# A four-layer convolution chain on one core: weight slices and sums at the begin reordered, side work spread over the slots, last image of the main stage by halves

## The chip, the core and the metric

The kernel runs on one core of a Trainium2 chip. The metric is the device time of one execution in microseconds (us). TensorE (PE) multiplies, VectorE (DVE) and ScalarE (ACT) do the elementwise work, GpSimd (POOL) does a few small chains, SyncE (SP) issues most of the DMAs. Each engine runs its own list of instructions in the order in which the code writes them, and waits on semaphores.

## The reference

The input x has 16 images of 32 channels and 28 x 28 pixels. Four layers follow each other.

```
def ternarize(w):
    delta = 0.7 * mean|w|;  mask = |w| > delta
    alpha = sum(|w| * mask) / sum(mask)
    return alpha * sign(w) * mask
# layer 0: 32 -> 192 -> 192 -> 32 channels
h = relu6(bn(conv1x1(x, ternarize(w1)), ...))
h = relu6(bn(conv3x3(h, ternarize(w2)), ...))
h = bn(conv1x1(h, ternarize(w3)), ...)
y = x + h
# layer 1: two 3x3 convolutions, input and weights rounded to 8 bits with a step from the
#          maximum over the whole tensor, batch norms, relu, residual
# layers 2 and 3: 3x3 convolution, bias, batch norm, relu; a whole channel of an image
#          is zeroed where its maximum is under 0.001
```

The mean of |w2| is a sum over 192 x 192 x 9 weights, and no weight of w2 can be made ternary before it is known. The step of each 8-bit rounding in layer 1 needs the maximum over all 16 images, so layer 1 can't start before the last image of layer 0 is done.

## The kernel before, in words

**Data.** Four images are stacked in the 128 partitions; c counts the four groups, g the image in a group, and j = 4c + g is an image of 0 to 15. The 192 hidden channels are two blocks, 0 to 127 ("a") and 128 to 191 ("b", 64 wide, of which two row sets share the 128 columns as a "pair"). `big` holds the raw weights of w2 (`w2ar` for the input channels 0 to 127, `w2br` for the other 64, once in each half of the partitions).

**Begin.** DMAs bring w2a in three slices, w2b, w1, w3, x and the batch-norm parameters. ACT sums |w2a| by slices (L684), then |w2b| (L687), and adds the three slice sums up (L690). PE sums over the partitions by a product with ones (`total`, L396). DVE derives the threshold (`thr_ready`), makes w2 ternary (`w2_rows`, `w2_transforms`, `w2_rest`) and forms the transformed weights wu and wub. POOL works out the batch-norm factors once the parameters land (`inv_ready`). The input is split exactly into three bf16 parts (`split` on DVE, `x_high` on ACT), and SP copies the parts of each image under each other (`spread`), so that one product over 96 rows is the expansion. Image 0 is expanded directly (L537).

**Main stage.** Each engine runs `slot(c, g)` 16 times. In a slot PE issues four quarters of the expansion of image j + 2 (`expand`, L421, all through PSUM bank 6, so that each has to wait until ACT has read the one before, `relu_exp`, L703), the outer row products of image j (`outer(0)`, `outer(3)`, L454), the middle ones of image j + 1 (`middle`, L444), and the pairs `pair_outer(j)` (L475) and `pair_middle(j+1)` (L464). In the first slot of a group it also projects the group before (`project`, L490). DVE's slot begins with `rows_03(j+1)` (L1061) and goes on with `seed_pair(j)` (L1081), the clamps of image j - 1 (`upper_a` L1086, `lower_a` L1091, `upper_b` L1096, `lower_b` L1101), the fixed-point split of image j + 2 (`grid` L1038, `fine` L1045/L1047), `seed_rows(j+1)` (L1072/L1073: they write the banks into which `outer` of the next slot accumulates) and `rows_12(j+2)` (L1055/L1056). ACT's slot is:

```
relu_exp(j+2, 0); relu_b(j-1); copy_y(j); [x_high of the next group]
relu_exp(j+2, 1); relu_exp(j+2, 2); coarse(j+2, 0)
relu_a(j); relu_exp(j+2, 3); copy_m1(j+1); coarse(j+2, 1); [add_shift(c) if g == 1]
```

Work that isn't any image's own is called **side work** below: the splits of groups 1 to 3, `w3_rest` (w3 made ternary), `scales` (the factor alpha), the maxima of the layer-1 to layer-3 weights (L1201 to L1204) with the transposes that spread them, and `integers` (L809/L813, the rounded weights of layer 1). Before, DVE does `w3_rest` and `split(1)` ahead of its first slot, and nearly all else behind its slots 0, 1 and 2. Slots 4 to 11 are a hardware loop.

**End of the main stage.** Slot 15 computes its outer rows and its pair. ACT reads both row blocks in one instruction (`relu_a`), DVE clamps the whole image, PE projects both halves of the pixels, and `residual` (L1108, L1111) adds x and takes maxima. Then `step(0)` finds the global maximum: DVE L1242, PE `largest` (L587), DVE L1244 to L1247, and layer 1 begins. `keep_warm` (L407) issues products whose result isn't used.

**Layers 1 to 3.** Two quantized 3x3 convolutions (L597), with `step(1)` between them, then two layers over stacked copies (L632). The order is written by hand throughout.

## Time and profile before

| what | us |
|---|---|
| median of 3 runs | 285.79 |
| those runs | 286.43, 285.79, 283.64 |
| the profiled execution's own time | 283.94 |
| its span in the profile | 282.1 |
| PE busy | 243.8 |
| DVE busy | 243.4 |
| ACT busy | 192.1 |
| POOL busy | 11.9 |

The span leaves out about 1.8 us of the profiled execution's own time. Busy time is a mean over very different stages: the main stage, from 33 to 207 us, has PE busy nearly all the time, while the begin and the turn to layer 1 are chains of short steps.

### The profile page before, as it was taken

The numbers are of one execution on the slowest core, as the hardware profiler recorded it, in microseconds if no ns is written. First come the engines' busy times: TensorE is split into PE (matmuls) and PEld (weight loads), VectorE is DVE, ScalarE is ACT, GpSimd is POOL, SyncE is SP. The second block draws the span as 40 slices with busy tenths as digits, with TensorE's granted clock in tenths as the row PEclk, the third lists the DMA queues.
The fourth block names the chain that finished last, engine by engine and source line by source line (L and its number), as shares of the span: only waits on it lengthen the run. The fifth ranks groups of instructions, "written<-read, shape, count | busy, mean of one in ns | idle before, by whom it ended". The sixth has DMA issues, their size and how long they took to land.

```text
span 282.1 us, 5680 instructions
## 1 busy us (share of the span) xinstructions
PE 243.8 (86%) x2138; PEld 132.1 (47%) x2138; DVE 243.4 (86%) x458; ACT 192.1 (68%) x283; POOL 11.9 (4%) x24
## 2 busy tenths in 40 slices
PE   0455979788999999999999999999977999789963
PEld 0222435344655455555455555455533555445531
DVE  6589996999999999999799999797658848999873
ACT  3686756587767578768378777778423728998942
POOL 6600000000000000000000000000000000000021
PEclk9999979999999999999999999999999999999998
DMA  7922003121200000000000000000000000275254
GB/s 209 281 75 73 1 14 75 28 59 36 50 2 1 2 0 3 0 2 0 0 0 0 0 0 0 1 2 0 2 0 2 0 0 4 59 163 109 62 149 171
DMA packets 6902, 11.55 MB, mean 41 GB/s; under 512 B 2144, under 2 KB 5216, under 8 KB 6880
## 3 DMA queue, kind: packets, MB, share of 16 engines
q1 hardware_dynamic: 6608, 10.77, 14.3%
q10 hardware_dynamic: 272, 0.49, 0.7%
q8 instruction: 14, 0.23, 0.3%
q14 instruction: 8, 0.07, 0.1%
HBM read 4.04 MB, written 1.61 MB: 20 GB/s over the span
## 4 chain that ended last, share of the span: by engine, by line
PE 61%; DVE 15%; DMA 7%; ACT 7%; issue 5%; SPq 4%; DVEq 0%; ACTq 0%
PE ps L454 14%; PE ps L444 14%; PE ps L475 8%; PE ps L464 7%; PE ps L597 4%; PE ps L632 3%; PE ps L421 3%; SPq L311 3%; DMA big<-big 3%; DMA big<-w2a_in 2%; PE ps L490 2%; DMA big<-part 2%; PE ps L537 1%; DVE ug L1038 1%; ACT ra L703 1%
## 5 line engine op out<-in xcount | busy, mean ns | idle before, releaser
L703 ACT ACTIVATE ra<-ps,bn 128x392 f32<-128x392 f32 x64 | 43.3, 677 | 28.7 <-PE ps L421 26.1
L725 ACT ACTIVATE hs<-ug,magic 128x784 f16<-128x784 f16 x32 | 30.2, 949 | 17.3 <-DVE ug L1038 17.3
L454 PE MATMUL ps<-vv,w2at 128*128 128x392 f16 x192 | 39.0, 338 | 0.5 <-DVE ps L1072 0.5
L444 PE MATMUL ps<-vv,wu 128*128 128x392 f16 x180 | 36.4, 336 | 0.0
L421 PE MATMUL ps<-xk,w1t 96*128 (+1 forms) x60 | 20.9, 348 | 11.9 <-ACT ra L703 11.9
L632 PE MATMUL ps<-big,wst 128*32 128x392 f16 (+2 forms) x576 | 25.5, 333 | 6.0 <-DMA big<-big 4.3
L597 PE MATMUL ps<-qi,wqi 128*128 128x392 bf16 x144 | 25.0, 333 | 1.0 <-ACT qi L838 1.0
L454 PEld LDWEIGHTS ps<-vv,w2at 128*128 128x128 f16 x192 | 18.4, 98 | 14.2 <-issue 1.6
L1061 DVE TENSOR_TENSOR vv<-hs 128x2520 f16<-128x2520 f16 x16 | 23.4, 1461 | 0.0
L444 PEld LDWEIGHTS ps<-vv,wu 128*128 128x128 f16 x180 | 17.5, 97 | 12.3 <-issue 0.4
L632 PEld LDWEIGHTS ps<-big,wst 128*32 128x32 f16 x576 | 14.7, 96 | 16.9 <-DMA big<-big 5.8
L454 PE MATMUL ps<-vv,w2bt 128*128 128x392 f16 x96 | 22.2, 340 | 0.0
L444 PE MATMUL ps<-vv,wub 128*128 128x392 f16 x90 | 20.4, 333 | 0.0
L475 PE MATMUL ps<-vv,w2at 128*64 128x392 f16 x192 | 19.7, 338 | 0.0
L1038 DVE TENSOR_SCALAR ug<-ra 128x784 f16<-128x784 f32 x32 | 17.9, 563 | 2.0 <-ACT ra L703 1.5
L597 PEld LDWEIGHTS ps<-qi,wqi 128*128 128x128 bf16 x144 | 13.8, 97 | 12.2 <-ACT qi L838 1.8
L464 PE MATMUL ps<-vv,wun 128*64 128x392 f16 x96 | 19.4, 336 | 0.0
L464 PE MATMUL ps<-vv,wu 128*64 128x392 f16 x96 | 19.4, 336 | 0.0
L870 ACT COPY big<-part 32x900 f16<-32x900 f16 x20 | 18.9, 943 | 0.5 <-DVE part L1373 0.2
L731 ACT ACTIVATE r2a<-ps,bn 128x784 f32<-128x784 f32 x16 | 16.1, 1003 | 4.4 <-PE ps L454 2.2
L421 PEld LDWEIGHTS ps<-xk,w1t 96*128 96x128 bf16 x60 | 5.8, 96 | 24.4 <-ACT ra L703 18.5
L838 ACT ACTIVATE qi<-ra,magic 128x420 bf16<-128x420 f32 (+1 forms) x16 | 9.0, 615 | 12.0 <-DVE ra L1254 12.0
(213 smaller groups left out, 461.5 us busy)
## 6 DMA issues: line engine op xcount, KB each, us to landing
xk<-xpart SPq DMA_DIRECT2D x45, 49.0 KB, 1.9
big<-big SPq DMA_DIRECT2D x4, 450.0 KB, 3.9
xin<-x_in SPq DMA_DIRECT2D x4, 392.0 KB, 7.2
big<-part SPq DMA_DIRECT2D x26, 56.2 KB, 2.4
y_out<-xin SPq DMA_DIRECT2D x3, 392.0 KB, 2.4
big<-w2a_in SPq DMA_DIRECT2D x3, 288.0 KB, 5.7
big<-w2b_in ACTq DMA_DIRECT2D x1, 432.0 KB, 5.9
big<-w2b_in SPq DMA_DIRECT2D x1, 432.0 KB, 6.8
```

Source lines behind the costliest of these rows:

```text
L421: nc.tensor.matmul(ps[:, bank, :HALF], (w1t[:, 0:P], w1t[:, P:P + 2 * HB])[two], xk[:, j, HALF * h:HALF * h + HALF], start=True, stop=True ...
L444: i = nc.tensor.matmul(ps[:, PBANK[k], :HALF], weights(s, k, dx, False), moving(s, k, dx, b), start=(s == 0 and dx == 0), stop=(s == 2 and ...
L454: i = nc.tensor.matmul(ps[:, PBANK[k], :HALF], weights(s, k, dx, False), moving(s, k, dx, b), start=False, stop=(s == 2 and dx == 2), skip ...
L464: i = nc.tensor.matmul(ps[HB * q:HB * q + HB, 4, :HALF], weights(s, k, dx, True), moving(s, k, dx, b), start=(s == 0 and dx == 0), stop=(s ...
L475: i = nc.tensor.matmul(ps[HB * q:HB * q + HB, 5, :HALF], weights(s, k, dx, True), moving(s, k, dx, b), start=False, stop=(s == 2 and dx == 2),
L597: i = nc.tensor.matmul(ps[:, bank + h, :HALF], wqi[:, k, t, :], qi[:, c, r0:r0 + HALF_ROWS, dx:dx + W], start=(t == 0), stop=(t == TAPS - 1))
L632: i = nc.tensor.matmul(ps[C * g:C * g + C, bank + h, :W * (rows.stop - rows.start)], wst[:, layer, C * t:C * t + C], kst[:, KBUF[layer][c] ...
L703: nc.scalar.activation(dst[:, HALF * h:HALF * h + HALF], ps[:, bank, :HALF], ACT.Relu, bias=bn[:, BSH, at:at + 1], scale=bn[:, BSC, at:at ...
L725: nc.scalar.activation(inner(hs[:, 2 * two]), img(ug[:, two, :]), ACT.Identity, bias=magic[:, 2:3]).then_inc(hh_ready, 1)
L870: ins = nc.scalar.copy(kst[C * k:C * k + C, KBUF[layer][c], g], part[C * g:C * g + C, layer, c % 2, k])
L1038: ts(ug[:, two, :], ra[:, two, :], CAP, GRID, ALU.min, ALU.add).then_inc(ug_ready, 1)
L1061: tt(vv[:, b, :, 0].rearrange("p s h w -> p s (h w)"), hs[:, :, 0:H, :].rearrange("p s h w -> p s (h w)"), hs[:, :, 2:H + 2, :].rearrange( ...
```

## The change

At the begin: x of group 0 is loaded first; the third slice of w2a goes through ACT's queue with w2b in three slices; w3 and the second copy of w2b wait until the first weights have landed, and x of groups 1 to 3 is loaded behind the spread of group 0. The halves of |w2b| are summed by ACT and DVE, and one product with ones takes five columns of partial sums, which DVE then adds up. The expansions of image 1 go to four banks and no longer wait for each other, and 18 products without use follow (`warm`). POOL clears `qi`, which DVE cleared before. ACT copies w1 (L841) and does its square sum of w2b ahead of `copy_m1(0)`.

In the main stage the loop is written out, and the side work is placed anew: `split` is two pieces, `split_first` (xrest) behind or in one slot and `split_second` (xpart) behind the next; `w3_rest` follows slot 1; the w3 scale (`scales_3`) is a step of its own; the weight maxima, the transposes and `split` of group 3 move to later slots, and the two `integers` stand ahead of slot 12 and behind it, where they stood behind slots 12 and 13.

At the end: the last pair's outer products go to bank 3, ahead of the last image's `outer(3)`, which is then PE's last; ACT and DVE treat the last image by halves; the small product for layer 1's scales moves ahead of `residual`. In layer 1 the last image of the first convolution has 18 and 10 rows in place of 14 and 14, and the clamp by 1e-8 becomes a ninth column of the maxima.

```diff
         @block.sync
+            sp.dma_start(xin[:, 0, :], x[:, 0, :]).then_inc(s_x[0], 16)
             for k in range(2):
                 dy = slice(3 * HID * k, 3 * HID * k + 3 * HID)
                 sp.dma_start(w2ar[:, dy], w2a[:, dy]).then_inc(s_w2a[k], 16)
-            sp.dma_start(xin[:, 0, :], x[:, 0, :]).then_inc(s_x[0], 16)
-            sp.dma_start(w2ar[:, 6 * HID:], w2a[:, 6 * HID:]).then_inc(s_w2a[2], 16)
+            sp.wait_ge(s_w2a[2], 16)
+            sp.wait_ge(s_w2b, 48)
             sp.dma_start(w3r[:, 0, :], w3[0:P]).then_inc(s_w3, 16)
...
         @block.tensor
-            pe.wait_ge(a_sum, 1)
-            total(3, 1, col[:, SUMS + 1:SUMS + 2], col[:, SB + 1:SB + 2])
+            pe.wait_ge(b_sum, 1)
+            pe.wait_ge(a_abs, 4)
+            total(3, 5, col[:, W2S:W2S + 5])
...
+            pe.wait_ge(thr_ready, 1)
+            pe.wait_ge(rb_ready, 2)
+            for n in range(4):
+                expand(1, n, bank=(0, 1, 5, 6)[n])
+            warm(WARM)
...
+            j = B - 1
+            outer(0, j, j % 2)
+            pair_outer(j, j % 2, bank=PBANK[2])
+            outer(3, j, j % 2)
             pe.wait_ge(rb_ready, 2 * B)
-            keep_warm(3, 4)
-            project(NCH - 1, 0, (0, 1), late=2)
-            project(NCH - 1, 1, (0, 1), bank=6, late=2)
-            keep_warm(4, 4)
-            project(NCH - 1, 0, (2, 3), late=2)
-            project(NCH - 1, 1, (2, 3), bank=6, late=2)
+            project(NCH - 1, 0, end=True)
+            project(NCH - 1, 1, (2, 3, 0, 1), bank=6, end=True)
...
         @block.scalar
+            slot(0, 0, first=True)
+            slot(0, 1, first=True, split=1)
+            x_high(2, 0)
+            slot(0, 2, first=True)
+            slot(0, 3, first=True, split=2)
+            act.wait_ge(pool_zeroed, 6)
+            slot(1, 0)
+            slot(1, 1)
+            x_high(3, 0)
+            slot(1, 2)
+            slot(1, 3, split=3)
+            slot(2, 0)
...
+            slot(2, 3)
             act.wait_ge(ws_ready, 1)
...
+            integers(0)
+            slot(NCH - 1, 0, last=True)
+            integers(1)
+            slot(NCH - 1, 1, last=True)
+            slot(NCH - 1, 2, last=True)
+            copy_y(B - 1)
+            relu_b(B - 2)
+            relu_half(B - 1, 0)
+            relu_b(B - 1, bank=PBANK[2])
+            relu_half(B - 1, 1)
...
         @block.vector
...
+            dve.wait_ge(s_w2b, 48)
+            nc.vector.tensor_reduce(c1(W2S + 4, HB), w2br[0:HB, TAPS * HID // 2:], AX.X, ALU.add,
+                                    apply_absolute_value=True).then_inc(b_sum, 1)
...
+            link(nc.vector.tensor_reduce(c1(TMP), ps[:, TOTAL_BANK[3], 24:29], AX.X, ALU.add))
...
-            w3_rest()
-            rows_12(1, 1)
-            split(1)
-            slot(0, 0, first=True)
-            split(2)
...
+            rows_12(1, 1)
+            slot(0, 0, first=True)
+            split_second(1)
+            slot(0, 1, first=True)
             w3_rest()
...
+            slot(0, 2, first=True)
+            split_first(2)
+            slot(0, 3, first=True)
+            split_second(2)
+            scales_3()
+            slot(1, 0)
+            slot(1, 1)
...
+            sizes(0)
+            slot(1, 2)
+            split_first(3)
+            slot(1, 3)
+            split_second(3)
+            slot(2, 0)
+            sizes(1)
...
+            seed_pair(j, bank=PBANK[2])
...
+            upper_half(j, g, 0)
+            lower_half(j, g, 0)
+            upper_b(j, g)
+            lower_b(j, g)
+            upper_half(j, g, 1)
+            lower_half(j, g, 1)
+            PQ, PC = 66, 68
+            link(tt(c1(PQ, w=2), c1(SW, w=2), bn[:, BSC, BNQ1:BNQ2 + 1], ALU.mult))
+            ts(c1(PQ, w=2), c1(PQ, w=2), 1.0 / XQ, None, ALU.mult)
             residual(NCH - 1, 0)
...
-                link(ts(c1(GM + k), c1(GM + k), 1e-8, None, ALU.max))
```

**DVE ahead of its first slot and in it.** The two splits' names are xrest and xpart, `seed_pair(0)` is the line `ps<-cy,ps`. Before:

```order
L1056 TENSOR_TENSOR vv<-hs 128x3x14x30
L970 TENSOR_TENSOR xrest<-xin 128x784
L972 TENSOR_TENSOR xpart<-xrest 128x784
L1061 TENSOR_TENSOR vv<-hs 128x3x840
L1081 TENSOR_TENSOR ps<-cy,ps 128x392
L1167 TENSOR_TENSOR col<-ps,col 128x1
```

Now, from the same place (L1137 is the old L1056, L1142 the old L1061):

```order
L1137 TENSOR_TENSOR vv<-hs 128x3x14x30
L1142 TENSOR_TENSOR vv<-hs 128x3x840
L1164 TENSOR_TENSOR ps<-cy,ps 128x392
L1259 TENSOR_TENSOR col<-ps,col 128x1
L1261 TENSOR_TENSOR col<-col,ps 128x1
L1262 TENSOR_SCALAR col<-ps 128x1
L1263 RECIPROCAL col<-col 128x1
L1264 TENSOR_TENSOR col<-col 128x1
L1270 TENSOR_SCALAR bn<-bn,col 128x2
L1119 TENSOR_SCALAR ug<-ra 128x784
L1041 TENSOR_TENSOR xrest<-xin 128x784
```

Both halves of the split of group 1, and `w3_rest`, no longer stand ahead of the first slot; one half stands inside it, the other behind it.

**ACT at the turn from slot 11 to slot 12.** `wqq` and `wqi` are the rounded weights of layer 1. Before, they stood behind slot 12:

```order
L709 COPY c1a<-ps 128x392
L725 ACTIVATE hs<-ug,magic 128x28x28
L809 ACTIVATE wqq<-wqr,magic,col 128x288
L813 ACTIVATE wqi<-wqq,magic 32x9x32 x4
L703 ACTIVATE ra<-ps,bn 128x392
```

Now the same pair of instructions stands ahead of slot 12 as well as behind it, and no longer behind slot 13:

```order
L757 COPY c1a<-ps 128x392
L773 ACTIVATE hs<-ug,magic 128x28x28
L872 ACTIVATE wqq<-wqr,magic,col 128x288
L876 ACTIVATE wqi<-wqq,magic 32x9x32 x4
L751 ACTIVATE ra<-ps,bn 128x392
```

**DVE at the end of the main stage.** `h2a` and `h2b` are the clamped last image. Before, the last lines up to the first `residual`:

```order
L1086 TENSOR_SCALAR h2a<-r2a 128x784
L1096 TENSOR_SCALAR h2b<-r2b 128x392
L1091 SCALAR_TENSOR_TENSOR h2a<-r2a,h2a 128x784
L1101 SCALAR_TENSOR_TENSOR h2b<-r2b,h2b 128x392
L1108 SCALAR_TENSOR_TENSOR y<-ps,bn,xin 128x14x28
```

Now:

```order
L1180 TENSOR_SCALAR h2a<-r2a 128x392
L1186 SCALAR_TENSOR_TENSOR h2a<-r2a,h2a 128x392
L1191 TENSOR_SCALAR h2b<-r2b 128x392
L1196 SCALAR_TENSOR_TENSOR h2b<-r2b,h2b 128x392
L1180 TENSOR_SCALAR h2a<-r2a 128x392
L1186 SCALAR_TENSOR_TENSOR h2a<-r2a,h2a 128x392
L1358 TENSOR_TENSOR col<-col,bn 128x2
L1359 TENSOR_SCALAR col<-col 128x2
L1203 SCALAR_TENSOR_TENSOR y<-ps,bn,xin 128x14x28
```

The first half and the pair's clamp stand ahead of the second half, which alone depends on PE's last products.

## Rows read from the trace of the kernel before

**Rows 1.** Windows: PE's slots 0, 3, 8: length, busy PE PEld DVE ACT POOL, PEclk, DMA

```profile
33.45:47.82 14.37, 12.41 (x82) 6.50 (x81) 12.00 (x33) 8.87 (x14) 0.00 (x0) 0.88 0.15 37
...
73.90:84.15 10.25, 10.25 (x78) 5.71 (x77) 9.87 (x20) 7.43 (x11) 0.00 (x0) 1.00 0.03 8
...
127.17:139.34 12.17, 12.17 (x111) 6.14 (x109) 10.03 (x16) 7.21 (x11) 0.00 (x0) 1.00 0.00 0
```

**Rows 2.** Chain that ended last, the begin (start, us, what)

```profile
2.10 6.92 DMA big<-w2a_in
```

**Rows 3.** Page, GB/s of the DMA engines in 40 slices of 7.05 us

```profile
GB/s 209 281 75 73 1 14 75 28 59 36 50 2 1 2 0 3 0 2 0 0 0 0 0 0 0 1 2 0 2 0 2 0 0 4 59 163 109 62 149 171
```

**Rows 4.** Timeline of the begin (start, us, engine, what, idle before and its end)

```profile
2.22 3.10 POOL L363 MEMSET part<- 128x3600 f32 x1
8.62 0.33 POOL L369 TENSOR_SCALAR bn<-par 128x9 f32<-128x9 f32 x1 [3.30 <-DMA par<-params_in]
9.73 1.63 ACT L687 ACTIVATE big<-big 64x1728 f32<-64x1728 f32 x1
13.10 0.23 DVE L981 TENSOR_SCALAR bn<-bn,col 128x2 f32<-128x2 f32 x1 [2.20 <-POOL bn L377]
13.68 0.80 DVE L1001 TENSOR_SCALAR big<-big,col 128x1152 f16<-128x1152 f32 x1
...
25.64 4.13 PE L553 MATMUL ps<-vv,wu 128*128 128x392 f16 x12
...
29.75 0.25 DVE L1015 TENSOR_SCALAR wubn<-wub 128x192 f16<-128x192 f16 x1
```

**Rows 5.** Timeline of DVE: `rows_03`, the entry of its slots 0, 3, 4 and 5

```profile
39.99 1.46 DVE L1061 TENSOR_TENSOR vv<-hs 128x2520 f16<-128x2520 f16 x1
77.13 1.45 DVE L1061 TENSOR_TENSOR vv<-hs 128x2520 f16<-128x2520 f16 x1
86.72 1.46 DVE L1061 TENSOR_TENSOR vv<-hs 128x2520 f16<-128x2520 f16 x1
97.92 1.46 DVE L1061 TENSOR_TENSOR vv<-hs 128x2520 f16<-128x2520 f16 x1
```

**Rows 6.** Timeline of ACT at the turn from slot 3 to slot 4

```profile
83.19 0.95 ACT L725 ACTIVATE hs<-ug,magic 128x784 f16<-128x784 f16 x1 [0.26 <-DVE ug L1038]
84.62 0.68 ACT L703 ACTIVATE ra<-ps,bn 128x392 f32<-128x392 f32 x1 [0.47 <-PE ps L421]
86.91 0.68 ACT L703 ACTIVATE ra<-ps,bn 128x392 f32<-128x392 f32 x1
```

**Rows 7.** Side work: groups of lines (busy, mean ns, idle), then timeline of ACT

```profile
L970 DVE TENSOR_TENSOR xrest<-xin 128x784 f32<-128x784 f32 x3 | 2.9, 963 | 0.0
...
48.27 0.83 ACT L677 COPY xpart<-xin 128x784 bf16<-128x784 bf16 x1
...
179.11 2.17 ACT L813 ACTIVATE wqi<-wqq,magic 32x288 bf16<-32x288 f32 x4
```

**Rows 8.** Windows: PE idle in slot 0, and 2 us later (columns as in Rows 1, PE alone)

```profile
35.35:37.12 1.77, 0.00 (x0) 1.00 0.00 0
39.00:40.00 1.00, 1.00 (x5) 0.50 0.00 0
```

**Rows 9.** Timeline of the end of the main stage

```profile
206.42 0.68 PE L475 MATMUL ps<-vv,w2bt 128*64 128x392 f16 x6
206.50 0.57 DVE L1086 TENSOR_SCALAR h2a<-r2a 128x784 f16<-128x784 f32 x1 [0.31 <-ACT r2a L731]
...
209.25 0.85 PE L490 MATMUL ps<-h2a,w3t 128*32 128x392 f16 x16 [1.55 <-DVE h2a L1091]
...
211.37 0.62 DVE L1108 SCALAR_TENSOR_TENSOR y<-ps,bn,xin 128x392 f32<-128x392 f32 x1 [1.78 <-PE ps L490]
...
214.19 0.46 PE L587 MATMUL ps<-ident,mx 128*128 128x128 f32 x2 [1.42 <-DVE mx L1242]
...
215.01 0.15 DVE L1245 TENSOR_SCALAR col<-col 128x1 f32<-128x1 f32 x1
```

More of the change, by code:

```diff
@@ L478, in pair_outer, with project @@
                 i.then_inc(convb_done, 1)
-            def project(c, h, steps=(0, 1, 2, 3), bank=7, late=1):
+            def project(c, h, steps=(0, 1, 2, 3), bank=7, end=False):
                 wait(pe, y0_ready, 2 * c + h if bank == 7 else 0)
@@ L658, in _ @@
             act.dma_start(w1r[:], w1).then_inc(s_w1, 16)
-            act.dma_start(w2br[0:HB, :], w2b).then_inc(s_w2b, 16)
             act.dma_start(par[:], params).then_inc(s_par, 16)
+            act.dma_start(w2ar[:, 6 * HID:], w2a[:, 6 * HID:]).then_inc(s_w2a[2], 16)
+            for k in range(3):
+                dy = slice(3 * HID * k, 3 * HID * k + 3 * HID)
+                act.dma_start(w2br[0:HB, dy], w2b[:, dy]).then_inc(s_w2b, 16)
             n = [0]
@@ L746, in add_shift, with slot @@
                                      bias=bn[:, BSH, BN3:BN3 + 1]).then_inc(xs_ready, 1)
-            def slot(c, g, first=False, last=False):
+            def slot(c, g, first=False, last=False, split=None):
                 j = c * G + g
                 begin = first and g == 0
-                end = last and g == G - 1
                 ahead = not last or g < G - 2
@@ L764, in slot @@
                     copy_y(j)
-                if first and g < NCH - 1:
-                    x_high(g + 1, 1)
+                if split is not None:
+                    x_high(split, 1)
                 if ahead:
@@ L769, in slot @@
                     relu_exp(j + 2, 2)
+                if begin:
+                    copy_m1(j + 1)
+                if ahead:
                     coarse(j + 2, 0)
                 if begin:
-                    copy_m1(j + 1)
+                    relu_exp(j + 2, 3)
                     act.wait_ge(bn_ready, 1)
                 relu_a(j)
-                if ahead:
+                if ahead and not begin:
                     relu_exp(j + 2, 3)
-                if not end and not begin:
+                if not begin:
                     copy_m1(j + 1)
@@ L782, in slot @@
                     add_shift(c)
+            x_high(0, 1)
+            act.wait_ge(w1_ready, 1)
+            for k in (1, 2):
+                i = nc.scalar.copy(w1t[C * k:C * k + C, :], w1t[0:C, :])
+            i.then_inc(w1_ready, 1)
             act.wait_ge(bn1_ready, 1)
@@ L1115, in slot @@
                 begin = first and g == 0
-                end = last and g == G - 1
                 ahead = not last or g < G - 2
-                if not end:
-                    rows_03(j + 1, (g + 1) % 2)
+                rows_03(j + 1, (g + 1) % 2)
                 seed_pair(j)
@@ L1139, in slot @@
                     grid(j + 2, 1)
-                if not end:
-                    seed_rows(j + 1)
+                seed_rows(j + 1)
                 if g == 0 and not first:
@@ L1205, in _ @@
             i.then_inc(mxt_go, 1)
-            slot(0, 1, first=True)
-            split(3)
+            slot(2, 1)
             dve.wait_ge(mxt_done, 1)
```

338 lines of the change are left out of this document (188 added, 150 removed).

## The prediction

> **What bounds the kernel now.** I read the windows per slot first. From slot 3 on PE is busy without a break: slot 3 takes 10.25 us with 10.25 busy, slot 8, which also projects, 12.17 of 12.17 [rows 1]. There a faster DVE or ACT gains nothing. Slots 0 to 2 are different: slot 0 takes 14.37 with 12.41 busy, at a mean clock of 0.88, and DVE is busy 12.00 against 9.87 in slot 3 [rows 1]. They are long because DVE does side work there. Against three slots of 10.27 the stage loses some 9.6 us (slots 0 to 2 last from 33.45 to 73.90, 40.45 in all [rows 1]). The begin, before PE's slot 0 at 33.45, is a chain: the last slice of w2a lands at 9.0 [rows 2], ACT sums, PE adds over partitions, DVE gets the threshold and starts on w2 at 13.68; the last transformed weight is written at 30.0 [rows 4]. The end is a chain too: PE's last product of the stage ends at 207.1, `largest` stands at 214.19, with only 0.85-us pieces of PE between [rows 9].
>
> So three things can move the time: when the first slot begins, how much side work PE has to wait for, and the 7.1 us at the end.
>
> **The begin.** What must land for the threshold is x of group 0 (0.40 MB), w2a (0.88), one copy of w2b (0.44) and small things, 1.77 MB. Before, it shared the engines with w3, the second w2b and 1.2 MB of x. The page shows 209 GB/s in the first slice of 7.05 us (1.47 MB) and 281 in the second [rows 3], so 1.77 MB are through at 7.05 + 0.30/0.281 = 8.1 us. Then ACT sums the last slice, a third of the columns of L687 (1.63) and so about 0.7 with the read-out, and half of w2b, 0.8 + 0.2: to 10.0, where L687 ended at 11.4 [rows 4]. From there to DVE's first step on w2 it took 2.3 us (to 13.68): ACT's sum of sums, two products, six short DVE steps. Now the sum of sums and one product are gone and the sums of |w3| stand elsewhere, some 1.1 less, but the expansion's scale, worked out in ACT's shadow before, and one more DVE step come in, 0.8: 2.0, so DVE starts on w2 at 12.0, 1.7 earlier. POOL must not be late: it clears `part` until 5.3 and now `qi` (half as many elements, half of 3.10), to 6.9; its chain from 8.62 to 13.0 lasts 4.4 [rows 4], so 11.3. Hence the gain lies between 0.7 (slice still at 9.0) and 2.1 (POOL ends last). The second w2b and groups 1 to 3 land later, but their readers come after 22 us; a DMA of SP is late only if `spread(0)` moves past the end of image 0's expansion, which it meets within a microsecond.
>
> The Trainium skill, page "DMA: Bandwidth & Descriptors", section "Anatomy of one DMA", gives about 2 us fixed plus bytes at 436 GB/s. By that the weights would be there at some 6.8 us, and the gain would be POOL's bound, 2.1; the slices of the page of the profile, at 209 and 281 GB/s, don't agree, and I go by them.
>
> Between there and the first slot, image 0's expansion starts as soon as the product is out (it stood behind it before), which saves DVE a short wait, and the two sums of |w3| cost 0.35 in the middle of the w2 chain. The transformed weights end at 28.3 in place of 30.0. PE then has six products and `pair_middle` to do, 2.6 us at the fast level: its slot 0 starts at 30.9. DVE entered slot 0 at 39.99 [rows 5]; off that come `split(1)`, two instructions of 0.96 [rows 7], `w3_rest`, eight short steps at some 0.19 with their gaps (0.15 each, [rows 9]), and the 1.7: 34.9.
>
> **The clock.** PE's 12 products of image 0 take 4.13 us at 25.64 [rows 4], 0.33 each, against 0.17 in full slots (78 products in 10.25 us, 36 of them two at a time [rows 1]): the 1.2 GHz level. The 18 products (6 us, from 16.5 to 22.5) end where DVE has image 0's rows ready, and should bring the 2.4 GHz level: 2 us of PE saved, but DVE's w2b chain follows until 28.3, so the saving turns into idle time. In that idle time of 3 us the level may fall back: a pause of 1.77 us at 35.35 is followed by a granted clock of 0.50 at 39 us [rows 8]. The Trainium skill, page "TensorE: Matmul & The Clock Gate", section "What's actually happening", says an idle array drops to half rate; that speaks against this placement of the useless products. By the row PE would lose up to 1.7 us between 28 and 33. I count it at nothing, since DVE, entering at 34.9, is the later one in slot 0; with its cover gone it costs 1.7.
>
> **The slots.** Two rules, both from the turn 3 to 4. DVE without side work takes 9.6 us a slot (77.13 to 86.72 [rows 5]); a `residual`, 1.2, comes on top in the first two slots of groups 1 to 3. PE's slot j+1 can't keep pace before DVE's entry to slot j plus 6.5: ACT's `coarse` ends 7.0 after the entry (83.19 + 0.95 - 77.13 [rows 5, 6]), then ACT needs 2.97 from 84.62 to 87.59 for four steps before PE's third quarter of the expansion, which stands 3.47 into PE's slot [rows 6]. What ACT does in between comes on top: `x_high` 0.85, `add_shift` the same size (I take 0.93), `integers` 2.17 and the rounding ahead of it, 2.8 [rows 7]. DVE's seeds give the same bound. Entries of DVE, with the side work in brackets: slot 1 at 45.8 (clamps absent, six scale steps 1.15, split 1.9, a short wait for ACT), 2 at 56.9 (w3 1.5), 3 at 67.5 (0.97), 4 at 79.0 (0.97, 0.95), 5 at 89.8, 6 at 101.5 (two maxima over 288 columns, estimated at 0.9 from 0.96 for 784), 7 at 112.1, 8 at 122.7 (0.97 each), 9 at 134.8 (1.3), 10 at 146.1 (0.5), 11 at 156.9 (1.15). PE, at 10.3 a slot and 12.2 in slots 4, 8 and 12: slot 1 at 42.5; slot 2 not at 53.2 but at 45.8 + 6.5 + 0.93 + 0.83 = 54.1; slot 3 at 64.4; 4 at 75.2 (with the w3 product, 0.5); 5 at 87.4; 6 at 99.3 for 97.7 (residual, `add_shift`, `x_high`); 7 at 109.6; 8 at 119.9; 9 at 132.1; 10 at 143.4 for 142.4; 11 at 154.0; slot 12 at 156.9 + 6.5 + 2.8 = 166.2 for 164.3, because `integers(0)` now stands ahead of it, where ACT has no pause that long. Before it was 170.16: eight full slots of 10.27 and two of 12.2 after 73.90, less what is rounded. From there PE is full again. **Gain in the main stage 4.0**, of which 2.5 are the begin's. If no side work delayed PE at all, slot 12 would start at 160.7, a gain of 9.4; that is the upper bound. The lower one is the begin's 0.7 alone. I take 4.0, because both rules come from full slots.
>
> The loop written out costs nothing: slots outside and inside it take the same time [rows 1].
>
> **The end.** PE's work is the same and ends at the same distance, with `outer(3)` of image 15 last. Counted from that end: ACT reads 392 columns 0.7; DVE clamps 0.4 and 0.6 (half of the full-image instructions), to 1.7; two short steps 0.4, to 2.1; two residuals as before. Before, the first residual stood 4.3 behind PE's end and `largest` another 2.8 [rows 9]; now 2.1 and 2.6, since the two short steps no longer stand between. 4.7 in place of 7.1: **2.4**, between 1.8 and 2.8. The project's first half needs the pair's clamp, which is done 0.1 after PE's end. Clamping by 1e-8 goes from both maximum chains, 0.19 each (a step of 0.15 with its gap [rows 9]): 0.4. The last image's 18 and 10 rows shorten the last ACT and DVE pieces of the first convolution by some 0.1 each: 0.2.
>
> **Sum.** 4.0 + 2.4 + 0.4 + 0.2 = 7.0. The profiled execution took 283.94 by itself (span 282.1), so 276.9; the runs shown stand at 283.64, 285.79 and 286.43, and with the profiled one their mean is 285.0. I put the forecast at 285.0 - 7.0 = 278.0; against the median alone it would be 278.8.
>
> **Rivals.** First, the side work is all covered: ACT's and DVE's bounds are looser than the turn 3 to 4 tells, and PE is the only bound from slot 1. Then the stage gains up to 9.4, and the time is 272.6 to 275. For it: DVE idles a little in every full slot, 9.87 busy of 10.25. Against: with DVE entering four microseconds behind PE, ACT has no pause left. Chance 0.17.
>
> Second, DVE lags more than I count and only begin and end pay, 1.7 + 3.0: 280.3. For it: 12 slots carry extra steps, each with a semaphore. Chance 0.15.
>
> Third, the clock: the level stays at 1.2 GHz through slot 0 and its 18 products of `outer`, 1.5 more than counted, and reaches DVE by `seed_rows(1)`: 279.5. Chance 0.08.
>
> Fourth, the change doesn't do what it says: the slices land no earlier, as ACT's queue issues the third slice of w2a behind w1 and the parameters. Gain of the begin 0.7, time 279.0. Chance 0.07.
>
> Fifth, slower: the side work now lies in slots where PE had no break. Put off there are the last split piece of group 2, the w3 scale, the maxima, the split of group 3 and the weight scales, 0.97 + 0.95 + 2.2 + 1.9 + 0.5 + 1.15 = 7.7 us of DVE. It decides from a DVE slot of 10.27 upward, PE's own length: then each of them is paid in full while slots 0 to 2 stay as they are, 285.0 + 7.7 - 4.7 = 288.0. DVE's 9.6 speaks against it. Chance 0.03.
>
> The forecast itself, 276.3 to 279.9 by its bounds, has 0.50. The range from 273.5 to 281.5 leaves out the best part of the first rival, the slower one, and some error of the base. A measurement of this kernel tells about 1% from no change, here 2.9 us. Faster by more than that (below 282.9): 0.9; within 0.07; slower 0.03.
>
> **What would show it.** DVE starts on w2 near 12.0; PE's slot 0 near 31, DVE's entry near 35; the products of image 0 at 0.17 each; PE waits for ACT (the expansion) at slots 2, 6, 10 and 12 by one to two microseconds and not elsewhere; slot 12 at 166; `largest` 4.7 behind PE's last `outer`. It is wrong if PE waits in most slots, or if DVE's slot without side work isn't 9.6.

## The result, and the profile after

| what | us |
|---|---|
| the changed kernel, median of 4 runs | 275.84 (276.95, 275.83, 274.72, 275.85) |
| the kernel before, median of 4 runs beside it | 285.99 (283.64 to 286.43) |
| ratio, 95% interval | 0.966 (0.962 to 0.970) |
| the profiled execution of the changed kernel | 276.95, span 275.0 |

The kernel is faster by 3.4%. Forecast were 278.0 (273.5 to 281.5) and faster. The kernel was run six more times later; over all ten runs its median is 276.20, and that is the number with which the experiments below are compared.

The page of the changed kernel, busy share, clock and GB/s in 40 slices of 6.9 us:

```profile
PE   0585889999999999999999997999988999889973
DVE  5899979999999999999899998799678858999893
PEclk9999599999999999999999999999999999999998
GB/s 235 90 108 215 9 1 0 54 37 0 2 22 68 1 0 4 0 2 66 23 2 4 0 0 0 4 2 0 2 0 1 2 0 0 61 153 109 102 132 175
```

The loads are seen to be in another order: 235 GB/s in the first slice, 90 in the second, 215 in the fourth, where the page of before has 209 and 281 and then falls to 75 [rows 3]. The row of the clock has a digit 5 near 30 us; the row of before has a 7 near 38 us, and 9 near 30.

Windows of PE's slots 0, 3, 8 and 12, then PE's pause at the begin and the stretch behind it (length, busy PE PEld DVE ACT POOL, clock, DMA):

```profile
33.45:45.45 12.00, 11.23 (x83) 6.33 (x81) 9.43 (x19) 6.65 (x10) 0.00 (x0) 0.96 0.00 1
67.10:78.02 10.92, 10.40 (x79) 5.70 (x78) 10.72 (x16) 7.96 (x12) 0.00 (x0) 1.00 0.01 2
121.84:133.99 12.15, 12.15 (x110) 6.15 (x109) 11.23 (x18) 7.42 (x11) 0.00 (x0) 1.00 0.20 50
165.41:179.47 14.06, 12.50 (x111) 6.13 (x109) 11.44 (x18) 12.09 (x21) 0.00 (x0) 1.00 0.01 2
25.15:28.30 3.15, 0.00 (x1) 0.01 (x1) 3.01 (x8) 1.61 (x3) 0.00 (x0) 0.88 0.28 72
30.00:34.00 4.00, 4.00 (x22) 1.71 (x21) 3.93 (x7) 2.51 (x5) 0.00 (x0) 0.50 0.03 6
```

Slot 0 lasts 12.00 in place of 14.37, slot 3 10.92 in place of 10.25, slot 8 the same [rows 1]. The side work has left the first slots and is seen in the later ones as DVE's 10.72 busy of 10.92. Slot 12 is now the worst: 14.06 with 12.50 busy, and PE waits in it for ACT, which is busy 12.09. PE's slot 0 starts at 33.45, to the hundredth where it stood before, although the last transformed weight came 1.8 us sooner: of the four microseconds from 30 to 34 all were at the granted clock of 0.50, the 1.2 GHz level.

Timeline of the begin and of slot 0 (start, us, engine, what, idle before):

```profile
8.79 0.92 ACT L734 ACTIVATE big<-big 64x864 f32<-64x864 f32 x1 [0.45 <-DMA big<-w2b_in]
...
11.93 0.81 DVE L1082 TENSOR_SCALAR big<-big,col 128x1152 f16<-128x1152 f32 x1
...
17.27 4.87 PE L572 MATMUL ps<-part 128*128 128x392 f16 x18
...
22.91 2.24 PE L589 MATMUL ps<-vv,wu 128*128 128x392 f16 x12 [0.43 <-DVE vv L1137]
...
27.99 0.25 DVE L1096 TENSOR_SCALAR wubn<-wub 128x192 f16<-128x192 f16 x1
...
28.30 2.14 PE L589 MATMUL ps<-vv,wub 128*128 128x392 f16 x6 [3.15 <-DVE wubn L1096]
...
34.96 1.46 DVE L1142 TENSOR_TENSOR vv<-hs 128x2520 f16<-128x2520 f16 x1
...
37.72 0.16 DVE L1259 TENSOR_TENSOR col<-ps,col 128x1 f32<-128x1 f32 x1 [0.82 <-PE ps L411]
...
41.57 0.98 DVE L1128 SCALAR_TENSOR_TENSOR hs<-ra,hs 128x784 f16<-128x784 f32 x1 [1.30 <-ACT hs L773]
...
47.63 1.46 DVE L1142 TENSOR_TENSOR vv<-hs 128x2520 f16<-128x2520 f16 x1
```

DVE starts on w2 at 11.93 (13.68 before [rows 4]), ends the transformed weights at 28.24 (30.0) and enters slot 0 at 34.96 (39.99 [rows 5]). The 12 products of image 0 take 2.24 us in place of 4.13, but behind them PE now idles 3.15 us until the last weights are there, where it idled 0.29 before. In slot 0 DVE waits twice: 0.82 us for PE's `total` (L411), which stands behind PE's first outer products, and 1.30 us for ACT's `coarse` (L773), ahead of which ACT has waited 2.66 and 1.05 us for PE's expansion.

Waits of PE, 33 to 203 us, in one line: 3.9 us in six pieces, two of them in slot 12 (total, number of waits, longest).

```profile
PE ps L438 <- ACT ra L751: 3.9, 6, 1.2
```

Timeline of the end of the main stage:

```profile
203.67 0.68 PE L471 MATMUL ps<-vv,w2bt 128*128 128x392 f16 x3
...
205.50 0.57 DVE L1186 SCALAR_TENSOR_TENSOR h2a<-r2a,h2a 128x392 f16<-128x392 f32 x1
...
206.12 0.52 PE L509 MATMUL ps<-h2a,w3t 128*32 128x392 f16 x8 [0.86 <-DVE h2a L1186]
...
206.26 0.63 DVE L1203 SCALAR_TENSOR_TENSOR y<-ps,bn,xin 128x392 f32<-128x392 f32 x1
...
208.95 0.46 PE L626 MATMUL ps<-ident,mx 128*128 128x128 f32 x2 [0.88 <-DVE mx L1368]
```

From PE's last outer product (204.35) to `largest` it is 4.6 us, where it was 7.1 [rows 9].

**Where the time came from**, by spans: before 282.1 in its profile, with its slot 13 at 182.3, `largest` at 214.2 and 67.9 behind that. The changed kernel's slot 13 stands at 179.5 in its first profile, but at 178.2, 178.5 and 179.1 in three others with the same begin and slots (below). So the stage gives 2.8 by the first and 3.7 by the mean of the three, the end 2.4 (from slot 13 to `largest` 31.9 before, 29.5 now), and the stretch behind the first maximum 1.9 to 2.1.

### The profile page after: what moved, and what is told of

Read it like the earlier page. It is cut to its first block, busy times and chain, and to the rows that moved or that the text cites. A ratio compares the mean times of both kernels' runs of the same rounds, so it can differ in the third digit from the quotient of the medians.

```text
span 275.0 us, 5586 instructions
## 1 busy us (share of the span) xinstructions
PE 245.5 (89%) x2151; PEld 133.5 (49%) x2151; DVE 244.4 (89%) x460; ACT 192.3 (70%) x285; POOL 14.2 (5%) x26
## 4 chain that ended last, share of the span: by engine, by line
PE 56%; DVE 19%; ACT 9%; issue 6%; DMA 6%; SPq 1%; ACTq 1%; DVEq 0%
PE ps L461 14%; PE ps L471 10%; PE ps L492 8%; PE ps L481 8%; PE ps L636 5%; PE ps L671 3%; PE ps L438 3%; DMA big<-big 3%; ACT ra L751 2%; DMA big<-w2b_in 2%; ACT hs L773 2%; PE ps L509 2%; PE ps L563 1%; DVE hs L1126 1%; DVE ug L1119 1%
## 5 line engine op out<-in xcount | busy, mean ns | idle before, releaser
L773 ACT ACTIVATE hs<-ug,magic 128x784 f16<-128x784 f16 x32 | 30.2, 949 | 12.6 <-DVE ug L1119 12.6
L636 PE MATMUL ps<-qi,wqi 128*128 128x392 bf16 (+2 forms) x144 | 25.0, 333 | 0.7 <-ACT qi L913 0.7
L438 PE MATMUL ps<-xk,w1t 96*128 96x392 bf16 x60 | 20.3, 349 | 5.1 <-ACT ra L751 5.0
L1142 DVE TENSOR_TENSOR vv<-hs 128x2520 f16<-128x2520 f16 x16 | 23.4, 1461 | 0.0
L481 PE MATMUL ps<-vv,wun 128*64 128x392 f16 x96 | 20.4, 349 | 0.0
L481 PE MATMUL ps<-vv,wu 128*64 128x392 f16 x96 | 20.3, 348 | 0.0
L779 ACT ACTIVATE r2a<-ps,bn 128x784 f32<-128x784 f32 x15 | 15.1, 1003 | 3.7 <-DVE h2a L1174 3.7
L1128 DVE SCALAR_TENSOR_TENSOR hs<-ra,hs 128x784 f16<-128x784 f32 x16 | 15.6, 972 | 1.3 <-ACT hs L773 1.3
L1126 DVE SCALAR_TENSOR_TENSOR hs<-ra,hs 64x784 f16<-64x784 f32 x16 | 15.6, 976 | 0.9
```

The lines of the kernel that those rows point to most:

```text
L438: nc.tensor.matmul(ps[:, bank, :HALF], (w1t[:, 0:P], w1t[:, P:P + 2 * HB])[two], xk[:, j, HALF * h:HALF * h + HALF], start=True, stop=True ...
L481: i = nc.tensor.matmul(ps[HB * q:HB * q + HB, 4, :HALF], weights(s, k, dx, True), moving(s, k, dx, b), start=(s == 0 and dx == 0), stop=(s ...
L636: i = nc.tensor.matmul(ps[:, bank + h, :W * rows], wqi[:, k, t, :], qi[:, c, r + dy:r + dy + rows, dx:dx + W], start=(t == 0), stop=(t == ...
L773: nc.scalar.activation(inner(hs[:, 2 * two]), img(ug[:, two, :]), ACT.Identity, bias=magic[:, 2:3]).then_inc(hh_ready, 1)
L1142: tt(vv[:, b, :, 0].rearrange("p s h w -> p s (h w)"), hs[:, :, 0:H, :].rearrange("p s h w -> p s (h w)"), hs[:, :, 2:H + 2, :].rearrange( ...
```

## The experiments

All but a0_same, c_both and b_before are single edits of the changed kernel. The table has all runs but the kernel before; ratios are to the runs of the kernel before on the same chip in the same group (medians 285.14, 285.22 and 286.03).

| kernel | median us | ratio, 95% interval | against 276.20 |
|---|---|---|---|
| a0_same | 276.60 | 0.971 (0.968 to 0.974) | +0.4 |
| t_bridge | 274.92 | 0.964 (0.961 to 0.967) | -1.3 |
| t_nowarm | 275.80 | 0.968 (0.964 to 0.972) | -0.4 |
| t_integers | 275.23 | 0.966 (0.963 to 0.969) | -1.0 |
| u_end | 278.69 | 0.977 (0.974 to 0.980) | +2.5 |
| u_side | 278.35 | 0.977 (0.974 to 0.980) | +2.2 |
| u_layer1 | 276.86 | 0.974 (0.971 to 0.977) | +0.7 |
| u_load | 278.77 | 0.979 (0.976 to 0.982) | +2.6 |
| c_both | 273.15 | 0.956 (0.953 to 0.959) | -3.1 |

### The same kernel again

> The changed kernel itself, unaltered, as the base for the others of this group on the same chip. Both theories: 274.7 to 277.0, ratio to the kernel before 0.962 to 0.970. Rival reading of its first profile (a fall of the clock in slot 0 is rare and the usual run has none): the mean granted clock is over 0.995 in most runs; the other reading (it falls in every run): 0.985 to 0.990 in most.

Six runs of 275.44 to 277.19, median 276.60, at mean clocks of 0.984 to 0.994. So the fall of the clock isn't rare: in all six runs the mean is under 0.995, and the second of my two readings is nearer. Of the first four runs of this kernel one had a mean of 0.999, and it was the fastest of the ten (274.72). The mean counts falls at the kernel's end as well, so only a profile tells where one lies. The fall at the begin isn't equally long: in the first profile it slows the six products behind the pause and all of `pair_middle` (28.3 to 33.4 us), here it comes only behind the six products, and DVE goes from slot 0 to slot 1 in 11.52 us, 35.69 to 47.21, where it took 12.67. It doesn't wait for `total`, and 1.06 us for `coarse`. The ratio, 0.971, lies just above the 0.970 that was expected.

### 18 more products in the pause: t_bridge

```diff
                 if s == 2:
+                    warm(18)
                     pe.wait_ge(w2_ready, 3)
```

> Edit: 18 more products without use between the second and the third group of image 0's middle products, where PE of the changed kernel idles 3.15 us (25.15 to 28.30) ahead of a stretch of 6.8 us at a granted clock of 0.50. Theory A (DVE leads in slot 0, so the clock's fall costs nothing): within 0.5 us of the changed kernel. Theory B (the half-rate stretch holds up seed_rows(1) and so DVE's entry to slot 1, 47.63 where 45.8 was forecast, and that is carried to the end): PE's slot 0 starts at 31.5 or earlier with the clock at 1.00, DVE's slot 1 near 46, and the time is 1 to 2.5 us less.

1.3 us less than the ten runs, clocks 0.996 to 1.000. Theory B holds. Timeline of PE and DVE in this kernel:

```profile
26.50 3.15 PE L572 MATMUL ps<-part 128*128 128x392 f16 x18
...
29.80 1.22 PE L590 MATMUL ps<-vv,wub 128*128 128x392 f16 x6 [0.16 <-DVE wubn L1097]
...
36.41 1.46 DVE L1143 TENSOR_TENSOR vv<-hs 128x2520 f16<-128x2520 f16 x1
...
47.00 1.46 DVE L1143 TENSOR_TENSOR vv<-hs 128x2520 f16<-128x2520 f16 x1
```

The six products behind the pause take 1.22 us in place of 2.14, and slot 0 of DVE 10.59 in place of 12.67 and 11.52. The theory's outcome holds, its path doesn't: DVE waits 0.10 us ahead of `seed_rows(1)` here and 0.11 in the changed kernel. What goes away is the wait for `total` (0.82) and nearly all of the wait for `coarse` (1.30, here 0.14). My figures for the absolute times missed: slot 0 at 32.63, slot 1 of DVE at 47.00. In this execution the second slice of w2a landed late (ACT began on it at 9.37, in the first profile of the changed kernel at 6.91), which set the whole begin back by 1.5; the other five spans are 272.7 to 273.2 beside 274.1 here. `c_both`, below, shows the same edit with an early slice.

### No warm products at all: t_nowarm

```diff
-WARM = 18
+WARM = 0
```

> Edit: the 18 products without use are taken out. Theory A (they buy image 0's products at 0.17 each, but that time turns into idle time): image 0's 12 products take 0.33 each again, and the time is within 0.5 us of the changed kernel. Theory B (without them the clock rises later and slot 0 is slower still): 1 to 2 us more. Theory C (they cause the fall, since without them PE isn't granted the full rate before its pause and the climb comes once, in slot 0, as before): time 0 to 1 less.

0.4 less than the ten runs, 0.8 less than a0_same, 0.9 more than t_bridge. The timeline of PE:

```profile
23.11 4.08 PE L589 MATMUL ps<-vv,wu 128*128 128x392 f16 x12 [2.55 <-DVE vv L1137]
28.49 2.14 PE L589 MATMUL ps<-vv,wub 128*128 128x392 f16 x6 [1.31 <-DVE wubn L1096]
```

The 12 products are slow again and end 1.3 us ahead of the last weights: they were never on the path. PE climbs once, at about 32 us, as before, and its slot 0 starts at 32.98, 0.47 ahead of the first profile of the changed kernel. So the 18 products of the change bought nothing that these runs can tell: what they saved turned into a pause, and the pause cost the level. That is the first half of theory A and the mechanism of theory C; of B there is nothing.

### The end as it was: u_end

```diff
             outer(0, j, j % 2)
-            pair_outer(j, j % 2, bank=PBANK[2])
             outer(3, j, j % 2)
+            pair_outer(j, j % 2)
...
-            seed_pair(j, bank=PBANK[2])
+            seed_pair(j)
...
-            upper_half(j, g, 0)
-            lower_half(j, g, 0)
+            upper_a(j, g)
             upper_b(j, g)
+            lower_a(j, g)
             lower_b(j, g)
...
```

> Edit: the end of the main stage alone is put back as it was (last image whole, outer(3) ahead of its pair, keep-warm products, the small product for layer 1's scales behind residual). Theory A (the end's 2.4 us are a chain that nothing else covers): largest stands 7.1 behind PE's last product in place of 4.6, and the time is 2.3 to 2.7 more. Theory B (part of it came from the begin or the slots, or is taken back by layer 1): 0 to 1.5 more.

+2.5 by medians. The slots are those of the changed kernel (slot 13 at 178.47), `largest` stands at 210.35, 31.88 behind it; in a0_same it is 29.48 (179.06 to 208.54). That is 2.4, the sum of the prediction. Theory A. The waits that come back, from the timeline of PE in this kernel:

```profile
205.41 0.85 PE L628 MATMUL ps<-h2a,w3t 128*32 128x392 f16 x16 [1.55 <-DVE h2a L1189]
...
210.35 0.46 PE L642 MATMUL ps<-ident,mx 128*128 128x128 f32 x2 [1.42 <-DVE mx L1381]
```

### Side work at its old places: u_side

```diff
+            w3_rest()
             rows_12(1, 1)
-            slot(0, 0, first=True)
-            split_second(1)
-            slot(0, 1, first=True)
-            w3_rest()
+            split_first(1)
+            split_second(1)
+            slot(0, 0, first=True)
+            scales_3()
+            split_first(2)
+            split_second(2)
...
+            slot(0, 1, first=True)
+            split_first(3)
+            split_second(3)
```

> Edit: the side work alone is put back to its old places (w3 made ternary and the split of group 1 ahead of DVE's slot 0, nearly all else behind slots 0 to 2; x_high and xrest on ACT and DVE likewise). The begin, the bridge of 18 products and the end stay new. Theory A (my sum: 2.5 of the stage's gain are the begin's and 1.5 the placing of side work): 1 to 2.5 us more. Theory B (the placing is what carries the gain, because the begin's is eaten by PE's unchanged slot-0 start of 33.45): 3 to 5 more. Theory C (side work costs the same wherever it stands): within 0.5.

+2.2, by theory A. The windows of slots 0, 1, 2 and 12:

```profile
32.85:45.48 12.63, 11.40 (x86) 6.64 (x85) 11.10 (x31) 7.29 (x11) 0.00 (x0) 1.00 0.15 38
45.48:60.50 15.02, 12.14 (x79) 6.33 (x78) 14.54 (x31) 9.46 (x15) 0.00 (x0) 0.89 0.20 51
60.50:72.38 11.88, 10.75 (x79) 6.02 (x78) 11.57 (x19) 9.18 (x14) 0.00 (x0) 1.00 0.19 46
168.45:181.05 12.60, 12.32 (x110) 6.15 (x109) 10.09 (x17) 10.69 (x18) 0.00 (x0) 1.00 0.01 2
```

Slot 1 grows to 15.02, with one wait of 2.88 us for ACT in it. Slot 13 stands at 181.05: with the new begin and the old places 1.3 us ahead of the kernel before, and 2.5 behind the mean of the three. The time fits theory A's range, but not its split. One thing isn't put back: `integers` stands ahead of slot 12 here as well. So the split is cleaner at the start of slot 12, where the three profiles stand at 164.5 in the mean, this kernel at 168.45 and the kernel before at 170.16: the begin is worth 1.7 there and the places 3.9. In slot 12 itself the kernel before took 12.15, this one 12.60 and the changed one 14.06, which leaves 1.3 and 2.5 at slot 13. All of these are single executions, and the three profiles differ by 0.9 at either place. That slot 12 lasts only 12.60 fits my second rule: DVE enters its slot 11 at 159.29, 1.1 us behind PE, and 159.29 + 6.5 + 2.8 is 168.6, where PE is anyway; in the changed kernel DVE enters 2.8 behind PE (157.99 and 155.16).

### The loads in their old order: u_load

```diff
-            sp.dma_start(xin[:, 0, :], x[:, 0, :]).then_inc(s_x[0], 16)
             for k in range(2):
...
-            sp.wait_ge(s_w2a[2], 16)
-            sp.wait_ge(s_w2b, 48)
+            sp.dma_start(xin[:, 0, :], x[:, 0, :]).then_inc(s_x[0], 16)
+            sp.dma_start(w2ar[:, 6 * HID:], w2a[:, 6 * HID:]).then_inc(s_w2a[2], 16)
...
-            act.dma_start(w2ar[:, 6 * HID:], w2a[:, 6 * HID:]).then_inc(s_w2a[2], 16)
...
```

> Edit: the order of the loads alone is put back (x of group 0 behind two slices of w2a, third slice in SP's queue, w3, the second w2b and x of groups 1 to 3 issued at once and waiting for nothing). The halves of |w2b|, the single product, the bridge of 18, the slots and the end stay new. Theory A (what must land first decides): DVE starts on w2 1 to 1.7 us later than at 11.9, and the time is 0.9 to 1.7 more. Theory B (queues share the engines as they did, and the new begin is the sums' and the product's): DVE's start within 0.4, time within 0.5.

+2.2 beside a0_same of the same group, more than either theory had. The timeline of ACT and DVE:

```profile
8.89 0.84 ACT L736 COPY xpart<-xin 128x784 bf16<-128x784 bf16 x1 [3.78 <-DMA xin<-x_in]
9.64 0.68 ACT L724 ACTIVATE big<-big 128x576 f32<-128x576 f32 x1
...
11.71 1.03 DVE L1050 TENSOR_REDUCE col<-big 64x1 f32<-64x864 f32 x1
...
14.70 0.81 DVE L1080 TENSOR_SCALAR big<-big,col 128x1152 f16<-128x1152 f32 x1
```

DVE's start on w2 goes from 12.57 (a0_same) to 14.70, which is later than before the change (13.68 [rows 4]). Two things add up to these 2.1. The last slice of w2b lands at 11.19 here and at 9.54 in a0_same, 1.65 later. The rest is in the lines: ACT copies x, and DVE works on it, ahead of the sums, and x comes only at 8.87, so that DVE reaches its half of w2b at 11.71 and ACT its own at 11.65. New order of loads and new lists of the engines belong together; the old loads with the new lists make a later begin than either kernel has.

### Layer 1 as it was: u_layer1

```diff
-QROWS = [(HALF_ROWS, HALF_ROWS)] * (NCH - 1) + [(18, 10)]
+QROWS = [(HALF_ROWS, HALF_ROWS)] * NCH
...
+                link(ts(c1(GM + k), c1(GM + k), 1e-8, None, ALU.max))
```

> Edit: layer 1 alone is put back (last image of the first convolution 14 and 14 rows, clamp by 1e-8 as an instruction of its own in both maximum chains). Theory A (my sum): 0.4 to 0.7 us more than the changed kernel. Theory B (the 1.46 us that the stretch behind the second maximum lost in the profiled run come from here): 1.2 to 1.8 more, and PE again waits 4.3 us for the stacked copies of layers 2 and 3.

+0.7 against the ten runs, +0.3 against a0_same. From `largest` to the end of the span it is 66.5 us here (207.69 to 274.2) and 65.9 in a0_same (208.54 to 274.4): 0.65, theory A. PE's last wait for a stacked copy stays at 1.56 here, so the long one of the kernel before isn't layer 1's doing.

### integers behind slots 12 and 13: t_integers

```diff
+            slot(NCH - 1, 0, last=True)
             act.wait_ge(ws_ready, 1)
             integers(0)
-            slot(NCH - 1, 0, last=True)
+            slot(NCH - 1, 1, last=True)
             integers(1)
-            slot(NCH - 1, 1, last=True)
             slot(NCH - 1, 2, last=True)
```

> Edit: the two steps integers(0) and integers(1) stand behind slots 12 and 13 on ACT again, in place of ahead of slot 12 and behind it. Theory A (the 1.18 + 0.39 us that PE waits for ACT in slot 12 are added time, as my second rule has it): 1.0 to 1.6 us less than the changed kernel. Theory B (it comes back as a wait in slot 13, since ACT has no pause of 2.8 us anywhere in slots 12 and 13): within 0.5. Theory C (integers(1) behind slot 13 holds up relu_b and the end): 0.5 to 1.5 more.

-1.0 against the ten runs, -1.4 against a0_same. The window of slot 12:

```profile
167.47:179.62 12.15, 12.15 (x110) 6.15 (x108) 11.28 (x18) 10.05 (x16) 0.00 (x0) 1.00 0.00 1
```

12.15 in place of 14.06, PE busy throughout, and no wait in slot 13: `largest` follows slot 13 by 29.49, as in a0_same (29.48). Theory A, and a little more than its figure, 1.9 by the trace, since the longer slot 12 also has 0.35 more of PE's busy time in it (12.50 against 12.15) beside its waits of 1.57. Behind slot 12 ACT still comes to wait for PE once the casts are through (0.62 and 0.49 us), and behind slot 13 there is no image left to expand.

### Both gains together: c_both

The edits of t_bridge and t_integers in one kernel.

> Edit: the two changes that gained by themselves together: 18 more products without use ahead of the third group of image 0's middle products, and integers behind slots 12 and 13. If the gains add up (1.3 and 1.4 us by medians, 1.0 and 1.9 by the slots' starts): 273.3 to 274.3 us, PE's slot 13 near 175.5 when the loads land as early as in the changed kernel's first profile. Rival: the second is partly the first's (DVE, earlier in every slot, leaves less wait at slot 12): 274.3 to 275.2.

273.15 (272.92 to 273.52), ratio 0.956 (0.953 to 0.959): 3.1 us less than the changed kernel. The edits add up and a little more, 0.15 below what was expected; the kernel before stood higher in this group too (286.03), and in the profile ACT could start on the second slice of w2a at 6.93, the early case. The timeline and the windows of slots 0 and 12:

```profile
28.68 1.22 PE L590 MATMUL ps<-vv,wub 128*128 128x392 f16 x6 [0.16 <-DVE wubn L1097]
...
35.28 1.46 DVE L1143 TENSOR_TENSOR vv<-hs 128x2520 f16<-128x2520 f16 x1
...
45.87 1.46 DVE L1143 TENSOR_TENSOR vv<-hs 128x2520 f16<-128x2520 f16 x1
```

```profile
31.50:43.17 11.67, 10.90 (x83) 6.22 (x81) 11.15 (x20) 7.69 (x12) 0.00 (x0) 1.00 0.00 1
...
163.41:175.56 12.15, 12.15 (x110) 6.15 (x109) 11.28 (x18) 10.06 (x16) 0.00 (x0) 1.00 0.00 1
```

Slot 0 starts at 31.50, DVE enters slot 1 at 45.87 (forecast for the changed kernel: 30.9 and 45.8), slot 13 at 175.56. The six runs lie within 0.6 us; those of the changed kernel spread over 2.5.

### The kernel before, a second profile: b_before

> The kernel before, unaltered, for a second profile. Question: is the stretch behind the first maximum, 67.9 us in its profile against 65.8 to 66.1 in seven profiles with the new layer 1, and 66.5 in the one with the old layer 1, long by the kernel or by one execution? If by one execution (the last stacked copy's first half took 3.27 us there and 1.96 in the others): 66.3 to 66.8 this time. If by the kernel: 67.6 to 68.1 again, with the last wait of PE at 2.5 or more.

Neither number: 70.3 us behind the first maximum (214.44 to 284.7), more than in its first profile. But the cause is the kernel's, not one execution's. The last wait of PE, in its timeline, and the window of the products behind it:

```profile
265.88 3.24 PE L632 MATMUL ps<-big,wst 128*32 128x392 f16 x72 [0.64 <-DVE big L1333]
272.07 7.95 PE L632 MATMUL ps<-big,wst 128*32 128x392 f16 x144 [2.95 <-DMA big<-big]
```

```profile
272.07:280.02 7.95, 7.95 (x144) 4.33 (x144) 3.85 (x8) 2.13 (x3) 1.85 (x2) 0.79 0.29 111
```

The same 144 products, in a0_same:

```profile
263.39 6.30 PE L671 MATMUL ps<-big,wst 128*32 128x392 f16 x144 [1.52 <-DMA big<-big]
```

PE waits 2.70 and 2.95 us in the two profiles of the kernel before, and 1.2 to 1.6 in the ten profiles of the changed kernel and its variants. The 56-KB transfer ahead of the last stacked copy takes 3.27 and 3.51 there, and 1.95 or 1.96 in the ten. Behind the wait of 2.95 the granted clock fell, to a mean of 0.79, and the last products took 1.65 more.

The layer-1 part of the change, the end of the main stage, the places of side work and the order of the loads aren't the reason: u_layer1, u_end, u_side and u_load have the short transfer too (1.95 or 1.96). The DMA packets of the trace show what is. Besides the kernel's own queue, q1, there is a queue q8 that the profile calls instruction, with packets of 16 KB. From the DMA view of the kernel before, 263.88 to 267.14 us, its slow transfer:

```profile
q1 hardware_dynamic: 140, 0.17, 21.7%
q8 instruction: 1, 0.02, 2.2%
big<-part SPq DMA_DIRECT2D x1, 56.2 KB, 3.3
```

And of a0_same, 256.97 to 258.93 us, the same transfer:

```profile
q1 hardware_dynamic: 140, 0.17, 35.9%
big<-part SPq DMA_DIRECT2D x1, 56.2 KB, 2.0
```

In the kernel before the q8 packet runs from 264.96 to 266.12 us. All packets of the transfer but three have started by 265.54, and the three start at 266.10, 266.30 and 266.48, as soon as it is through. In the second profile it is the same: 265.95 to 267.05, and three packets at 267.04, 267.23 and 267.42. In none of the ten other profiles does a q8 packet fall into this transfer. It falls into the last stacked copy instead, which takes 4.0 to 4.5 us with it and 3.94 in both profiles of the kernel before without it. All ten have the loop written out, and 17 q8 packets in the span of the first where the kernel before has 14. So the longer program gets its pieces at other times, and one of them no longer hits this transfer. No run moved a q8 packet by itself; that the change of the program's length is what moved it is argued.

## Why the prediction was right, point by point

**The begin.** DVE's start on w2 (12.0, measured 11.93), the end of the weights (28.3, 28.24) and DVE's entry to slot 0 (34.9, 34.96) came out. That 12.0 came out is luck, since two errors cancel. The slices at 209 and 281 GB/s on the page of the profile gave 8.1 for the last bytes; ACT and DVE waited for w2b until 8.79 in the first profile, 9.57 in a0_same, and DVE until 10.84 in t_integers. On the other hand the sum of w2a's last slice, 0.7 in my chain, is done before w2b is there. So the weights land hardly earlier than before: the last of them at 9.02 there [rows 2], and in nine profiles with the new loads at 8.8 to 10.8, in the middle one at 9.1. What shortens the begin is the work behind the last byte: 4.7 us to DVE's start on w2 before (9.02 to 13.68), 3.2 now (8.77 to 11.93) and 3.0 in a0_same. The measured 11.93 is also the earliest of the nine; the latest is 14.10. The term that was mis-sized is what the begin is worth later: 2.5 at slot 12 was counted, and u_side has 1.7 there. The Trainium skill's formula in "DMA: Bandwidth & Descriptors", section "Anatomy of one DMA", is given for a single DMA on another path (SWDGE); carried over to these loads, the estimate by it was 6.8, and it agrees with none of these.

**The clock.** "I count it at nothing, since DVE, entering at 34.9, is the later one in slot 0" is the step that failed. The fall happened as [rows 8] and the Trainium skill's page "TensorE: Matmul & The Clock Gate", section "What's actually happening", had it: after 3.15 us of idle time the granted clock went to 0.50. DVE did enter later than PE, but inside slot 0 it waited 0.82 us for PE's `total` and 1.30 for ACT's `coarse`, both behind PE's late slot 0, and came to slot 1 at 47.63 in place of 45.8. Filling the pause brings DVE's slot 0 from 11.5 or 12.7 down to 10.59. In the whole time it is 1.3 us (t_bridge), close to the third rival's 1.5. So the cost of a rival with a chance of 0.08 came true, by another path than it named: the level was back at 2.4 GHz within the first products of slot 0, and `seed_rows(1)` waited only 0.11 us. It was outweighed by the rest.

**The slots.** Slot 13 was forecast at 178.4 (166.2 and 12.2) and stands at 179.47 in the first profile, 178.2 to 179.1 in the three others; the gain of 4.0 measures 2.8 and 3.7. Its split was wrong, and the errors are of opposite sign: at slot 12 the begin is worth 1.7 in place of 2.5 and the places 3.9 in place of 1.5, of which `integers` then takes back 1.9 inside slot 12. That the total came out near is in part luck. The first rule held: from DVE's slot 1 to its slot 11 it is 110.4 us (47.63 to 157.99) where 111.1 were forecast. The second held where it mattered: DVE's entry to slot 11 and 6.5 + 2.8 give 167.3 for slot 12; PE started it at 165.41 and then waited 1.18 and 0.39 inside it, 167.0 in all. Elsewhere it was too strict. In the list of PE's starts 53.2 and 154.0 are 0.4 and 0.3 more than 10.3 a slot gives, without effect, since other bounds decide at slots 2 and 12. PE waited in slots 0, 1, 3, 7 and 12; what was forecast for the start of slot 2 came inside slot 1, and the waits ahead of slots 6 and 10 didn't come, though PE lost 0.5 in each of slots 3 and 7.

**The end.** 2.4 was the term; 2.4 by the first profile and by the traces of u_end against a0_same, 2.5 by medians.

**Layer 1.** 0.6 was the term; 0.65 by the traces of u_layer1.

**What the sum didn't have.** The terms measure 3.7, 2.4 and 0.65, 6.8 in all, and 7.0 was predicted. The medians are 8.6 apart for a0_same and its group, 10.2 in the result's own runs, and 9.0 between 285.2 and 276.2. 1.4 us of the rest is the stretch behind the first maximum, 67.9 against 66.5 with the same layer 1: the last stacked copy comes later in the kernel before, because the transfer ahead of it meets a packet of q8 (b_before). A further part is the clock behind that wait, 1.65 in the second profile of the kernel before. The prediction has neither: it took the loop written out as costing nothing, by the lengths of slots, and didn't look at when the program's pieces are loaded. The time of 278.0 was 1.8 too high for this, and the range held it.

**The rivals.** That all side work is covered (0.17) isn't so: PE still waits 3.9 us, and t_integers won 1.9 of it back. That only begin and end pay (0.15) isn't so either, as the places give 2.5. That the slices land no earlier (0.07) is nearly so, 9.02 before and 8.8 to 10.8 now, but its price isn't: the begin gained 1.8 in the first profile and 1.1 in a0_same all the same, by the shorter work behind them. u_load doesn't speak against it, since it undoes the order under the new lists alone. The slower rival had slots 0 to 2 stay as long as they were; they went from 40.45 to 33.65 us (33.45 to 67.10).

## What to carry to other kernels

Products without use are worth something where the real ones behind them end a chain; here they made early ones fast that had 1.3 us to spare, and opened a pause after which PE ran three to six microseconds at the lower level. Put them into the last pause ahead of the dense stretch, and count what the slow products hold up on other engines, not whether that engine starts later. When side work is spread, look where the engine that carries it has idle time left: the same two steps of ACT cost 0.45 with DVE entering 1.1 us behind PE, 1.9 with DVE 2.8 behind, and nothing one slot later. Don't count a load's new place as a gain before the landing of its last byte is seen: here the begin got shorter by the work behind the last byte, not by an earlier byte.
